# A fused transformer kernel: the score stream of its rotary attention set seven beats ahead, with SyncE's step and the fill reordered

## What is computed

```python
def attn_a(x):                    # causal, 16 heads of 8
    q, k, v = split(x @ c_attn_w + c_attn_b)
    attn = softmax(where(causal, q @ k.T / sqrt(8), min))
    # heads 0 to 2: weights of one region of tokens times 1.6, normed again
    return (attn @ v) @ c_proj_w + c_proj_b

def attn_b(x):                    # no mask; rotary q and k
    q, k, v = x @ Wq.T + bq, x @ Wk.T + bk, x @ Wv.T + bv
    q, k = rope(q, k)
    return softmax(q @ k.T / sqrt(8)) @ v @ Wo.T + bo

def ffn(x):
    h = silu(x @ w1.T * s1) * (x @ w2.T * s2)
    h = gelu(h @ h1.T * s3)
    h = gelu(h @ h2.T * s4)
    return h @ w3.T * s5

x = x + attn_a(norm(x)); x = x + ffn(norm(x))
x = x + attn_b(norm(x)); x = x + ffn(norm(x))
```

## Time and profile before

| | us |
|---|---|
| median of three runs | 2063.32 |
| lowest, highest | 2062.24, 2064.73 |
| the profiled execution | 2065.22 |
| its span, first to last instruction | 2063.5 |
| TensorE busy in the span | 1888.6 (92%) |
| VectorE busy | 1702.8 (83%) |
| ScalarE busy | 1478.0 (72%) |
| GpSimd busy | 1175.8 (57%) |
| mean granted TensorE clock | 0.962 |

### The profile page before, as it was taken

How to read it: one execution, slowest core, us unless ns; L and a number is a source line. 1 busy time by engine, 2 the same in 40 slices (tenths; PEclk the granted TensorE clock), 3 DMA queues, 4 the chain that set the end, 5 groups by cost and what they waited for, 6 DMA issues and landing times.

```text
span 2063.5 us, 42740 instructions
## 1 busy us (share of the span) xinstructions
PE 1888.6 (92%) x16132; PEld 966.2 (47%) x16132; DVE 1702.8 (83%) x2312; ACT 1478.0 (72%) x2641; POOL 1175.8 (57%) x1615
## 2 busy tenths in 40 slices
PE   3899999999889999986899999999999989999998
PEld 1333444444357777764222222222222227777776
DVE  4889898898658888876899999999999918888883
ACT  1478788788756666652698888888888876666665
POOL 6777788877446555677444454454553015555654
PEclk6799999999989999998799999999999989999999
DMA  7455656655110000014334444444444010000000
...
DMA packets 107892, 144.81 MB, mean 70 GB/s; under 512 B 19105, under 2 KB 87458, under 8 KB 101538
## 3 DMA queue, kind: packets, MB, share of 16 engines
...
## 4 chain that ended last, share of the span: by engine, by line
PE 59%; POOL 15%; issue 8%; ACT 8%; DVE 6%; DMA 2%; SPq 1%; POOLq 0%; another core or an unknown queue 0%; ACTq 0%; DVEq 0%
PE ps_score L1446 21%; PE ps_out L1065 12%; PE ps_score L1007 7%; ACT prob L993 6%; PE ps_max L1446 5%; PE ps_max L1025 5%; DVE negmax L882 3%; POOL xhat L324 3%; POOL prob L728 3%; PE ps_out L1446 3%; PE ps_max L1106 2%; POOL rstd L318 2%; POOL rest L693 1%; ACT o_raw L956 1%; POOL parts L700 1%
## 5 line engine op out<-in xcount | busy, mean ns | idle before, releaser
L993 ACT ACTIVATE prob<-ps_score 128x512 f32<-128x512 f32 x1664 | 900.4, 598 | 171.8 <-PE ps_score L1007 151.4
L882 DVE TENSOR_REDUCE negmax<-ps_max 128x2 f32<-128x1024 f32 (+1 forms) x896 | 905.6, 1066 | 90.7 <-PE ps_max L1042 47.9
L1065 PE MATMUL ps_out<-prob,v_aug 128*9 128x256 f32 (+2 forms) x6656 | 508.9, 386 | 30.9 <-ACT o_raw L956 20.4
L1446 PE MATMUL ps_score<-h,w_hi 128*128 128x512 f32 x2048 | 502.8, 399 | 9.4 <-POOL h L1224 8.2
L1446 PEld LDWEIGHTS ps_score<-h,w_hi 128*128 128x128 f32 x2048 | 383.3, 189 | 104.3 <-POOL h L1224 10.8
L1025 PE MATMUL ps_max<-stack_k,stack_q 48*128 48x512 bf16 (+3 forms) x2048 | 342.6, 353 | 46.6 <-DVE negmax L882 29.3
L1007 PE MATMUL ps_score<-stack_q,stack_k 50*128 50x512 bf16 (+3 forms) x2048 | 351.6, 347 | 31.0 <-ACT prob L993 23.1
L1212 POOL TENSOR_TENSOR h<-h3f,h 128x512 fp32r<-128x512 f32 x128 | 192.5, 1514 | 127.9 <-ACT h L1358 127.8
L728 POOL TENSOR_SCALAR_AFFINE_SELECT prob<-prob 128x256 f32<-128x256 f32 (+1 forms) x448 | 187.8, 440 | 117.7 <-ACT prob L993 117.3
L1065 PEld LDWEIGHTS ps_out<-prob,v_aug 128*9 128x9 f32 x6656 | 105.8, 89 | 306.0 <-ACT prob L993 153.9
L1007 PEld LDWEIGHTS ps_score<-stack_q,stack_k 50*128 50x128 bf16 x2048 | 103.7, 93 | 273.1 <-ACT prob L993 201.6
...
## 6 DMA issues: line engine op xcount, KB each, us to landing
d_stack<-parts SPq DMA_DIRECT2D x64, 384.0 KB, 2.6
stack_q<-d_stack SPq DMA_DIRECT2D x64, 384.0 KB, 5.7
stack_k<-d_stack SPq DMA_DIRECT2D x64, 384.0 KB, 6.0
...
d_stack<-parts SPq DMA_DIRECT2D x64, 128.0 KB, 2.7
o_num<-o_raw SPq DMA_DIRECT2D x128, 64.0 KB
o_rden<-d_rden SPq DMA_DIRECT2D x128, 64.0 KB
turned<-qf SPq DMA_DIRECT2D x64, 128.0 KB, 2.4
```

What stands on the lines that cost most here:

```text
L882: last = dve.tensor_reduce(m["negmax"][:, t, :, p], banks[:, :, at:at + w], AX.X, ALU.max, negate=True)
L993: act.activation(prob(b, i)[:, o], act_bank("score", 2 * i + o), ACT.Exp).then_inc(s["prob"], 1)
L1065: last = pe.matmul(m["ps_out"][32 * g:32 * g + HD + 1, out:out + w], m["v_aug"][b % VALUES][:, j, 4 * G + g, :], prob(b, beat)[:, g % 2, l ...
L1446: mm = pe.matmul(to, w[:, cols], moving(part), start=begin and i == 0, stop=last and i == len(pairs) - 1)
```

## The change

A number "ahead" is added to both tables: 0 for the causal stage, 7 for the rotary one. `ahead(n, i)` turns a beat of a step into the one seven later; scores, exponentials, value products and the copies of the sums are now taken from there, while maxima, linear products and transposes keep their beats. The scores of an entry start at beat 25 of the step before, its half 1 is reached at beat 9, and the copies of the sums stand at beats 5, 13, 21 and 29 in place of 12, 20, 28 and (of the next step) 4.

Fifteen places in ROTARY_AT are moved with it, among them "nm1" 3 to 2, "nm0" 23 to 18, "xT" 19 to 20, "q" 23 to 24. The rotary stage gets its own order for SyncE (`sync_rotary`). In the fill, GpSimd's last two instructions on q of entry 0 go behind the four low parts of layer three, the norm of entry 2 ahead of k of entry 1; VectorE projects k of entry 0 earlier, makes its parts later, and takes the statistics of entry 2 earlier. The last step is cut so that the gates stand behind its scores, as before. Left out of the diff below are the mask of the causal stage, which takes the same function with 0, and places where only a name changes.

```diff
--- before.py
+++ after.py
...
-             "D_proj": 9, "A_nm1": 2, "A_nm0": 14, "A_xT": 10, "order": "MSWX"}
-ROTARY_AT = {"k": 3, "nm1": 3, "v": 15, "proj": 14, "xT": 19, "nm0": 23, "q": 23,
-             "weigh": (4, 5, 6, 7, 8, 9, 10, 11), "out": 12, "P_nm1": 8, "P_norm": 15, "P_v": 13, "P_bias": 15,
-             "P_q1": 27, "P_q2": 31, "P_k1": 9, "P_k2": 13, "P_nm0": 19, "P_o": 0, "D_stats": 16, "D_clear": 18,
-             "D_q": 24, "D_k": 4, "A_v": 16, "D_bias": 2, "D_inv": 15, "D_proj": 15, "A_nm1": 4,
-             "A_nm0": 24, "A_xT": 20, "order": "SMWX"}
+             "D_proj": 9, "A_nm1": 2, "A_nm0": 14, "A_xT": 10, "order": "MSWX", "ahead": 0}
+ROTARY_AT = {"k": 3, "nm1": 2, "v": 15, "proj": 14, "xT": 20, "nm0": 18, "q": 24,
+             "weigh": (4, 5, 6, 7, 8, 9, 10, 11), "out": 12, "P_nm1": 0, "P_norm": 14, "P_v": 13, "P_bias": 18,
+             "P_q1": 28, "P_q2": 31, "P_k1": 9, "P_k2": 13, "P_nm0": 16, "P_o": 0, "D_stats": 10, "D_clear": 18,
+             "D_q": 25, "D_k": 4, "A_v": 16, "D_bias": 2, "D_inv": 6, "D_proj": 15, "A_nm1": 3,
+             "A_nm0": 19, "A_xT": 21, "order": "SMWX", "ahead": 7}
...
@@ -433,6 +434,10 @@
         return 0 <= n - lag < B
+    def ahead(n, i):
+
+        return divmod(BEATS * n + i + AHEAD, BEATS)
+
     def prob(b, i):
...
@@ -440,7 +445,8 @@
     act_turns, dve_turns = [], []
     for i in range(BEATS):
-        act_turns += [("score", 2, 2 * i + o) for o in range(2)]
+        step, at = ahead(0, i)
+        act_turns += [("score", 2 - step, 2 * at + o) for o in range(2)]
         dve_turns += [("max", 1, i)]
         for name, lag in (("nm1", 2), ("nm0", 1), ("xT", -1)):
...
@@ -610,17 +616,41 @@
         swap(sp, 1, "k", 1)
         store(sp, 1, "stored_q", 0)
+    def sync_rotary(sp, n):
+
+        if on(n, 2):
+            aug(sp, 1, n - 2)
+        if on(n, 0) and not early("k", n):
+            swap(sp, n, "k", 1)
+        if on(n, 0):
+            load(sp, n, "stack_q", "stored_q", 0)
+        if on(n, 3):
+            store_reciprocals(sp, n - 3)
+            spread_reciprocals(sp, n - 3)
+        if on(n, 0):
+            store(sp, n, "stored_k", 1)
+            load(sp, n, "stack_k", "stored_k", 1)
+        if on(n, 1):
+            aug(sp, 0, n - 1)
+        if on(n, -1):
+            swap(sp, n + 1, "q", 0)
+        if on(n, 2):
+            numerators(sp, n - 2)
+        if on(n, -1):
+            store(sp, n + 1, "stored_q", 0)
+
     def sync(sp, n):
         if causal and n == B:
             sp.wait_ge(f["halved"], 3)
             sp.dma_start(m["d_flags"].rearrange("(p o) -> p o", o=1), m["flags"][:]).then_inc(f["flag_moved"], 16)
+        if rotary:
+            sync_rotary(sp, n)
+            return
         if n == 0:
             store(sp, n, "stored_k", 1)
         if on(n, 3):
             numerators(sp, n - 3)
-        if rotary and on(n, 0) and not early("k", n):
-            swap(sp, n, "k", 1)
         if on(n, 2):
             aug(sp, 1, n - 2)
...
-        if rotary and on(n, -1):
-            swap(sp, n + 1, "q", 0)
         if on(n, 3):
             spread_reciprocals(sp, n - 3)
...
@@ -793,9 +822,9 @@
         add_bias(pool, 0)
         pool.wait_ge(f["h3_hi"], count(FT, B))
         ones(pool, range(1, VALUES))
+        norm(pool, 2)
         high(pool, 1, "k", 1)
         middle_low(pool, 1, 1)
-        norm(pool, 2)
         negated_max_parts(pool, 0, 0)
         add_bias(pool, 1)
         high(pool, 2, "q", 0)
...
-                if i == AT["D_stats"]:
+                if i == AT["D_stats"] and not (rotary and n == 1):
                     statistics(dve, n + 1)
                 if i == AT["D_q"]:
...
+            step, k = ahead(n, i)
+            for lag, G in plan.out_due(k):
+                if on(step, lag):
+                    group_out(act, step - lag, G)
+            if not on(step, 2):
                 continue
-            b = n - 2
-
-            before, at = divmod(BEATS * b + i - PROBS, BEATS)
+            b = step - 2
+
+            before, at = divmod(BEATS * b + k - PROBS, BEATS)
             if before >= 0:
                 wait(act, s["pv"], count(BLOCKS, before, plan.block_of[at] + 1))
             for o in range(2):
-                act.wait_ge(s["score"], count(2 * BEATS, b, 2 * i + o + 1))
-                act.activation(prob(b, i)[:, o], act_bank("score", 2 * i + o), ACT.Exp).then_inc(s["prob"], 1)
-
-    def scores(pe, n, i):
-
-        b, c = n - 2, (n - 2) % STACKS
+                act.wait_ge(s["score"], count(2 * BEATS, b, 2 * k + o + 1))
+                act.activation(prob(b, k)[:, o], act_bank("score", 2 * k + o), ACT.Exp).then_inc(s["prob"], 1)
+
+    def scores(pe, n, b, i):
+
+        c = b % STACKS
         if i % (BEATS // 2) == 0:
             h = i // (BEATS // 2)
...
+            step, k = ahead(n, i)
             for part in AT["order"]:
-                if part == "S" and on(n, 2):
-                    scores(pe, n, i)
+                if part == "S" and on(step, 2):
+                    scores(pe, n, step - 2, k)
                 if part == "M" and on(n, 1):
                     maxes(pe, n, i)
-                for lag, k in plan.block_due(i):
-                    if part == "W" and on(n, lag):
-                        weigh(pe, n - lag, k)
+                for lag, block in plan.block_due(k):
+                    if part == "W" and on(step, lag):
+                        weigh(pe, step - lag, block)
                 if part == "X":
                     misc_work(pe, n, i)
...
             if r == B - 2:
                 low(pool, b, 2, range(FT))
                 fill["high"](pool, 0, "q", 0)
+                low(pool, b, 3, range(FT))
                 fill["middle_low"](pool, 0, 0)
-                low(pool, b, 3, range(FT))
             if r == B - 1:
                 low(pool, b, 2, range(FT))
...
                 normed(b + 2)
             if fill:
                 fill["project"](dve, 0, "q", 0)
-            split(dve, b + 1, 0)
             if fill:
                 fill["project"](dve, 0, "k", 1)
+            split(dve, b + 1, 0)
             split(dve, b + 1, 1)
             if r == 0:
...
                 add_y(dve, b - 1)
             gated(dve, b + 1, 2)
             split(dve, b + 1, 2)
-            if fill:
-                fill["parts_on_vector"](dve, 0, "k", 1)
             gated(dve, b + 1, 3)
             if r < B - 2:
                 xT_low(dve, b + 2)
             split(dve, b + 1, 3)
+            if fill:
+                fill["parts_on_vector"](dve, 0, "k", 1)
             if after is not None and r == B - 3:
                 after.parts["statistics"](dve, 0)
...
@@ -1338,6 +1368,7 @@
             return
         fill = after.parts
         after.vector(dve, 1, 0, 5)
+        fill["statistics"](dve, 2)
         fill["project"](dve, 1, "q", 0)
         after.vector(dve, 1, 5, 7)
...
@@ -1382,8 +1413,10 @@
             act.wait_ge(s["halved"], 2)
         before.scalar(act, B + 1, 0, 12)
         xT_high(act, first)
-        before.scalar(act, B + 1, 12)
+        scored = before.plan.beats - before.plan.at["ahead"]
+        before.scalar(act, B + 1, 12, scored)
         gate(act, first, 0)
+        before.scalar(act, B + 1, scored)
         before.scalar(act, B + 2)
         gate(act, first, 1)
         high(act, first, 0)
...
@@ -1474,9 +1507,11 @@
                 product(m[f"ps_{name}"][:, f % 2], slice(at, at + P), lambda part: xT[:, part],
                         True, True).then_inc(s[done], 1)
-        before.tensor(pe, B + 1, before.plan.beats - 4)
+        scored = before.plan.beats - before.plan.at["ahead"]
+        before.tensor(pe, B + 1, scored - 4, scored)
         pe.wait_ge(over["resid"], B - 2)
         gates(first, 0)
+        before.tensor(pe, B + 1, scored)
         before.tensor(pe, B + 2)
         gates(first, 1)
```

16 lines of the change are left out of this document (7 added, 9 removed).

## The result

The changed kernel takes **2172.85 us** (median of four runs, 2172.42 to 2173.69); the kernel before took 2064.03 in the same comparison (four runs). The ratio is 1.0529, 95% interval 1.0514 to 1.0543: slower by 109 us. The sign was forecast, the size was not: 2088, with a range up to 2108.

The account below looks back on a forecast made before the run. No engine but GpSimd has slack for a long wait, and o_num copies would now cause one. Steps +28.4, fill +5, drain -8.5 make +25 on the profiled 2065.2: 2090, less 1.9 for the median, 2088 us; range 2068 to 2108.

Parts of the forecast that it names:

- The mechanism: Rotary steps: group 0's copy at beat 5 waits for o_num copies, these for oT, oT for q; 2.64 us a step.
- Landing: Rotary steps: the last 64 KB o_num copy lands 2.24 us after its issue, as the 32 KB den copy did.
- The upper bound: Rotary steps: o_num copies land as slowly as swaps, 3.7 us, 1.46 more; 3.8 us a step, +46 in all.
- The clock: TensorE in rotary steps: the new wait, some 2.4 us, leaves the clock full as a 2.02 us wait did; cost nothing.
- Rival 3: Rotary steps: the clock falls in each, 2 us a step, +24, 2112 us in all; chance 0.10.
- busy time costs nothing: Rotary steps: instructions keep number and size, so only when buffers must be free changes; 0 us.
- The count of steps, 4 to 15: Rotary stage: the wait holds in steps 4 to 15, 12 x 2.37 = +28.4 us.
- The fill: Start of the rotary stage: later q and k of entry 0 delay the first maxima; +5 us, between 0 and +9.
- the wait changes its place: Fill: TensorE's 3.91 us wait for entry 2's normed input moves to entry 0's transposed maxima, its size unchanged.
- The drain: Last rotary step to the gates: seven fewer beats, less 3.6 us for the o_num chain; -8.5 us, between -12 and -7.
- Rivals 1 and 2: Rotary steps: first, copies free in time, 2055 us, chance 0.13; second, new wait replaces old ones, 2069 us, chance 0.12.

Follow-up runs that it names:

- experiment 1: Changed kernel, but GpSimd makes oT of an entry in the step before: 2082.61 us, ratio 1.0097 to the kernel before.
- experiment 4: Changed kernel, but each o_num copy of the rotary stage moves 256 of 512 columns, half the bytes: 2132.03 us, ratio 1.0336.
- experiment 2: Changed kernel, but the stores of q's parts stand behind the second maxima and the next step's swap of k: 2162.19 us, ratio 1.0492.
- experiments 2 and 3: Changed kernel with the stores of q's parts moved later (2162.19 us), or put back ahead of the sums (2173.92 us, ratio 1.0544).
- experiment 5: Changed kernel, but GpSimd makes oT ahead of its last two instructions on q: 2114.24 us, ratio 1.0260.
- experiment 10: Changed kernel with oT a step earlier, fill undone, half 1's transposed maxima at beat 3, output product at 18: 2060.95 us, ratio 1.0001.

## Why the prediction was right in sign and wrong in size

- **The mechanism** was right, and experiment 1 shows it: group 0's copy at beat 5, behind the o_num copies, behind oT, behind q. Without that wait 90 us are gone.
- **The step that failed: "Landing: the nearest row is the 32 KB den copy ... 2.24 later. I take that for 64 KB too."** It measured 5.0. One 32 KB copy alone doesn't price four copies of 64 KB that share a rate; experiment 4 moved it with the bytes, experiment 2 puts 0.9 of it on the stores behind. The stretch of the kernel before around its own o_num copies, 43 to 61 GB/s, held the missing part. As an estimate: 2.24 for the first 32 KB, as den took, and the other 224 KB at 50 GB/s, 4.5, make 6.7 us from the first issue. I had 4.7; experiments 2 and 3, with no stores behind, measured 6.65 and 6.69, the changed kernel 7.54. For half the bytes the same estimate gives 4.2, with 0.9 for the stores 5.1, and experiment 4 measured 5.03. The rate alone, 5 us from the first issue, would have been little better than what I took. The upper bound, taken from swaps at 3.7, was too low as well. The rest of the chain fits: oT 0.3 later than forecast, the product itself due 0.6 later.
- **The clock: "the sum has nothing for it".** It cost 25.6 us over the twelve steps, 2.1 each (1.77 in the one shown). Rival 3 had 2 a step, and held together with the forecast, which I had set apart from each other. The wait was twice as long as that from which I argued; but even near 2 us the clock falls in some steps (experiment 5). The Trainium skill (TensorE: Matmul & The Clock Gate, A second HAM failure mode: psum-queue depth-cycling), which the prediction set against the row, says that short idle spells between groups of matmuls can make the clock swing. That came nearer than the row, but not for its reason: what swings here comes behind one long wait and not behind small ones, and the step shown of experiment 1 keeps 1.00 with all its small waits.
- **"A step's instructions are the same in number and size, so busy time costs nothing"** missed 1.44 a step, 17 us, half of it TensorE's busy time and half new small waits, the largest of them 0.68 for VectorE at beat 12. Experiment 10 recovered 0.6 to 0.7 by letting the transposes share beats with linear products again. That ScalarE's copy of them is what such a product covers was argued and fits, but only the place was varied.
- **The count of steps, 4 to 15,** left out step 16, which has a wait of 2.14 at beat 5 and cost 4.2, and step 3 with 1.6.
- **The fill** was +9.7, just above its upper end. The load of stack_k was issued at 941.67 (forecast 942) and the maxima started at 948.87 (forecast 948); the 2 us of half clock behind the 7.33 us wait were not in it. Of the norm of entry 2 it was right that the wait changes its place and brings no gain; the wait also grew, from 3.91 to 5.50.
- **The drain** gave 5.1 and not 8.5: the same landing, 5.66 us of wait in place of the 3.6 taken back, and the half clock. Without the chain, in experiment 1, the last step to the gates took 36.7, 11.3 less than before the change.
- **Sum.** 55.4 + 25.6 + 17.3 = 98.3 of the steps' 98.4. With only the landing right, 2.8 more a step, the forecast would have been near 2122, outside the range and still 51 short; the half clock and the 1.44 are the larger part of that, and both were put at nothing.

Rivals 1 and 2 are out: the wait neither vanished nor stood in for others (0.42, 0.53, 0.64 and 0.42 us stand beside it).
